# Softmax row sums in an attention kernel: the last key tile of each half is added by VectorE instead of GpSimd

## The reference, cut to what matters

```python
att = jnp.einsum('bhqd,bhkd->bhqk', q, k) * scale     # 16 heads of 64, 1024 queries, 1024 keys
att = jax.nn.softmax(att, axis=-1)                    # divides by the sum of each row over all keys
out = jnp.einsum('bhqk,bhkd->bhqd', att, v)
out = jnp.einsum('bne,de->bnd', out, Wo) + bo
```

## Time and profile before

| what | value |
|---|---|
| median of three executions | 3461.38 us |
| the profiled execution | 3464.02 us |
| span of its trace, first to last instruction | 3462.3 us |
| granted TensorE clock, mean | 0.993 |
| busy: TensorE, GpSimd, VectorE, ScalarE | 98%, 81%, 72%, 47% of the span |

### The profile page before, as it was taken

The page is one execution under the profiler, slowest core; times in us unless marked ns, Lnnn a source line. Parts: engine busy times, 40 slices in busy tenths (PEclk is TensorE's granted clock), DMA queues, the critical chain, the costliest instruction groups (busy, mean ns, idle before and its releaser), DMA issues. The chain is left out here.

```text
span 3462.3 us, 61727 instructions
## 1 busy us (share of the span) xinstructions
PE 3399.4 (98%) x16978; PEld 2088.4 (60%) x16978; DVE 2505.0 (72%) x3133; ACT 1640.8 (47%) x3086; POOL 2794.0 (81%) x2378
## 2 busy tenths in 40 slices
PE   8999799999999999999999999999999999999998
PEld 6888555555555555555555555555555555555698
DVE  8999567777777777777777777777777777777655
ACT  5666344444444444444444444444444444444432
POOL 3333389999999999999999999999999999999511
PEclk9999899999999999999999999999999999999999
DMA  7887756777677777777777677777776677776587
GB/s 246 245 238 240 200 129 160 186 191 187 184 185 186 185 184 182 191 192 189 185 186 187 185 186 186 185 192 187 185 186 186 186 185 181 190 192 155 180 277 251
DMA packets 424594, 669.27 MB, mean 193 GB/s; under 512 B 63585, under 2 KB 229218, under 8 KB 424546
## 3 DMA queue, kind: packets, MB, share of 16 engines
q1 hardware_dynamic: 410210, 645.60, 67.8%
q0 software_dynamic: 14336, 23.08, 3.4%
HBM read 306.98 MB, written 126.12 MB: 125 GB/s over the span
## 5 line engine op out<-in xcount | busy, mean ns | idle before, releaser
L1265 ACT ACTIVATE probs<-psum 128x512 f32<-128x512 f32 x2048 | 1078.1, 604 | 1196.9 <-PE psum L963 1184.9
L1343 DVE TENSOR_REDUCE merged<-psum 128x1 fp32r<-128x1024 f32 x1024 | 1201.1, 1215 | 591.0 <-PE psum L988 585.5
L1597 POOL TENSOR_TENSOR sums<-sums,probs 128x512 f32<-128x512 f32 x762 | 974.3, 1279 | 60.3 <-ACT probs L1265 2.0
L1598 POOL TENSOR_TENSOR sums<-sums,probs 128x512 f32<-128x512 f32 x762 | 979.6, 1286 | 0.0
L1003 PE MATMUL psum<-probs,v_sb 128*64 128x512 f32 x4096 | 935.9, 599 | 0.0
L960 PE MATMUL psum<-q_full,k_full 128*128 128x512 f32 x2048 | 862.2, 421 | 2.5 <-DVE merged L1343 1.6
L963 PE MATMUL psum<-q_rest,k_rest 65*128 65x512 f32 x2048 | 812.3, 397 | 3.4 <-DMA q_rest<-turned 3.4
L1003 PEld LDWEIGHTS psum<-probs,v_sb 128*64 128x64 f32 x4096 | 271.4, 136 | 562.9 <-issue 483.5
L960 PEld LDWEIGHTS psum<-q_full,k_full 128*128 128x128 f32 x2048 | 388.0, 189 | 178.2 <-issue 73.6
L963 PEld LDWEIGHTS psum<-q_rest,k_rest 65*128 65x128 f32 x2048 | 390.1, 190 | 71.0 <-DMA q_rest<-turned 3.7
L1064 PE MATMUL psum<-x_t,w_qk 128*128 128x512 f32 x1536 | 407.9, 402 | 10.2 <-DVE merged L1343 5.9
(11 more groups left out here) (171 smaller groups left out, 3375.0 us busy)
## 6 DMA issues: line engine op xcount, KB each, us to landing
x_t<-xt SPq DMA_DIRECT2D x118, 1024.0 KB, 7.1
k_full<-high SPq DMA_DIRECT2D x256, 256.0 KB
v<-values SPq DMA_DIRECT2D x64, 512.0 KB, 3.3
w_qk<-wqk_parts SPq DMA_DIRECT2D x64, 512.0 KB
v_sb<-v SPq DMA_DIRECT2D x64, 512.0 KB, 5.4
q_full<-high SPq DMA_DIRECT2D x128, 256.0 KB
q_full<-low SPq DMA_DIRECT2D x128, 256.0 KB
k_rest<-low SPq DMA_DIRECT2D x128, 256.0 KB
```

Of the source, the lines that this page charges most:

```text
L1265: nc.scalar.activation(probs[:, kt, h, :], score_bank(j), ACT.Exp, scale=SCALE).then_inc(probs_ready, 1)
L1343: nc.vector.tensor_reduce(out=merged[:, q // GROUP, col:col + 1], in_=work[:, 2 * h:2 * h + 2, :].rearrange("p b c -> p (b c)"), axis=AX, ...
L1597: nc.gpsimd.tensor_tensor(total[:, 0, :], first[:, 0, :], probs[:, kt, 0, :], ALU.add)
L1598: nc.gpsimd.tensor_tensor(total[:, 1, :], first[:, 1, :], probs[:, kt, 1, :], ALU.add).then_inc(sums_added, 1)
```

## The change

GpSimd adds the key tiles 1 to 6 of each half (twelve tiles in a step). Key tile 7 is added by VectorE with one tensor_tensor of 128x1024 for both heads, in a new filler `ADD`, which increments a new counter `sums_full`. `ADD0` (half 0 of this step) stands in group 2 behind NORM1, just ahead of `reduce(s, 5)`; `ADD1` (half 1 of the step before) stands in group 0 behind `low_part`, ahead of `reduce(s, 0)`. `add_up`, ScalarE's overwriting of key tile 7, and SyncE's loads of the last stage wait for `sums_full`. The adds of half 1 of the last step stay as they were.

```diff
-FILLERS = (((), (), ("RECIP0", "RECIP1")),
+FILLERS = (((), ("ADD1",), ("RECIP0", "RECIP1")),
            (("RECIP2", "RECIP3"), ("RAW1",), ("TOKEN0", "TOKEN1", "TOKEN2")),
-           (("NORM0", "SILU0"), ("SILU1", "SILU2"), ("NORM1",)),
+           (("NORM0", "SILU0"), ("SILU1", "SILU2"), ("NORM1", "ADD0")),
            ((), ("RAW0",), ()))
...
+ADDS = KT - 2
...
         def add_up(s, par, fin):
...
-                pe.wait_ge(sums_added, 14 * s)
+                pe.wait_ge(sums_full, 2 * s)
...
         def exp(s, g, i, h):
...
-                added = 14 * s + max(kt, 1) - (0 if g >= 2 else 7)
+                if kt == KT - 1:
+                    counter, added = sums_full, 2 * s + g // 2
+                else:
+                    counter, added = sums_added, ADDS * (2 * s + g // 2 - 1) + max(kt, 1)
                 if not known(added, 1):
-                    act.wait_ge(sums_added, added)
+                    act.wait_ge(counter, added)
...
+            elif name.startswith("ADD"):
+                half = int(name[-1])
+                if is_step(s, NP) or not (fin if half else att):
+                    return
+                p = s - half
+                dve.wait_ge(probs_ready, SCORES * p + 16 * (half + 1))
+                dve.wait_ge(sums_added, ADDS * (2 * p + half + 1))
+                total = sums1[:] if half else sums0[:, par]
+                nc.vector.tensor_tensor(total, total, probs[:, KT - 1], ALU.add).then_inc(sums_full, 1)
...
             for half in range(2) if att else ():
-                for kt in range(1, KT):
+                for kt in range(1, KT - 1):
...
-                        pool.wait_ge(sums_added, 14 * s + 7 * half + kt - 1)
+                        pool.wait_ge(sums_added, ADDS * (2 * s + half) + kt - 1)
```

More of the change, by code:

```diff
@@ L897, in attention_stage @@
     sums_added = sem("sums_added")
+    sums_full = sem("sums_full")
     sum_filled = sem("sum_filled")
@@ L1010, in add_up @@
             if is_step(s, NP):
-                pe.wait_ge(sums_added, 14 * NP - 7)
+                pe.wait_ge(sums_full, 2 * NP - 1)
                 pe.wait_ge(last_sums, 7)
             else:
-                pe.wait_ge(sums_added, 14 * s)
+                pe.wait_ge(sums_full, 2 * s)
             for h in range(2):
@@ L1761, in step @@
                 sp.wait_ge(pv_done, 4 * NP)
-                sp.wait_ge(sums_added, 14 * NP - 7)
+                sp.wait_ge(sums_full, 2 * NP - 1)
                 sp.wait_ge(last_sums, 7)
```

## The result

The changed kernel takes 3589.34 us (median of four executions, 3586.29 to 3589.63), the kernel before 3462.27 us, the median of the three executions named ahead of the prediction and one of 5504.96 us. The ratio is 1.0366, 95% interval 1.0346 to 1.0387: 3.7% slower. The prediction was 3565 us in a range of 3520 to 3605.

What follows compares the result with a forecast made beforehand. TensorE was taken to bound the kernel, at 44.5 us a step. ADD0's 73 us, ADD1's 34 us and -3 us at the end made +104 us, so 3565 us (+3.0%), in a range of 3520 to 3605.

Steps and rivals of the forecast that it cites:

- TensorE sets the pace: Steps of the loop: TensorE never waits for GpSimd, so taking 5.1 us a step off GpSimd is worth 0.
- ADD0 costs 1.2 us a step: Ahead of reduce(s, 5): ADD0 waits for GpSimd's product, delaying the reduction and PJ of group 3; 61 x 1.2 = 73 us.
- ADD1 costs 0.55 us: Ahead of reduce(s, 0): ADD1 waits for the freed GpSimd's first add, delaying add_up's matmuls; 61 x 0.55 = 34 us.
- The end gives 3 us back: Step without projections and last step: 5.3 us can come back, less VectorE's extra add; 3 us taken as gain.
- A: Rival: ADD1 is hidden, ADD0 isn't, as their order hangs on 0.15 us; 3531 us, chance 0.12.
- B: Rival: the adds cost what they cost alone, ADD0 late by 0.7 us, ADD1 hidden; 3501 us, chance 0.08.
- C: Rival: each VectorE add takes 2.30 us, as one in the trace does; 3604 us, chance 0.10.
- D: Rival: no change that can be told (within 0.2%, 7 us), only the end's gain left; 3458 us, chance 0.04.
- E: Rival: faster, GpSimd sets the pace through the buffers of probs; up to 5.1 us a step, 3150 us, chance 0.02.
- the signs named ahead: Profile after: period 46.2 us, ADD0 near 1.75, ADD1 near 2.2, TensorE waits of 1.2 and 0.5, GpSimd idle 3 us.

Runs made afterwards that it cites:

- the relief alone: Kernel before, with key tile 7 of both halves in no row sum (GpSimd adds twelve tiles, VectorE none): 3456.77 us, ratio 0.9983.
- the gather moved: Changed kernel with only GpSimd's copy and gather of the counts moved behind its first key tile of half 0: 3575.08 us, ratio 1.0331.
- both adds moved: Changed kernel with ADD0 between reduce(s, 5) and low_part of group 3, and ADD1 ahead of low_part of group 0: 3461.29 us, ratio 1.000.
- ADD0 moved alone: Changed kernel with only ADD0 moved, to between reduce(s, 5) and low_part of group 3: 3706.03 us, ratio 1.0709.
- the products later: Changed kernel with the expert's three products on GpSimd one key tile later, ahead of tile 4 of half 1: 3657.58 us, ratio 1.0574.
- ADD0 of one head: Changed kernel with ADD0 for head 0 only (128x512), tile 7 of half 0 left out of head 1's sums: 3547.53 us, ratio 1.0258.
- ADD1 alone: Changed kernel, but GpSimd adds all seven tiles of half 0 and VectorE only key tile 7 of half 1: 3507.57 us, ratio 1.0133.

## Why the prediction was right, point by point

**TensorE sets the pace, GpSimd's relief is worth nothing in the loop.** Shown: with the relief alone the period stayed 44.5 us, with all adds off the path too.

**ADD0 costs 1.2 us a step.** Shown: 1.75 us long as worked out, PJ late by 1.12 us and 0.1 us more behind it; alone 77 us over the 61 periods, where the sum had 73. (That the whole time grew by just 73.5 is luck: the end gave 3.5 us back.) That PJ has no slack, and that the price is the rest of GpSimd's instruction and 1.09 us, were shown by a longer instruction (2.30 us, PJ later by 0.55) and a smaller add (1.22 us, PJ earlier by 0.54).

**ADD1 costs 0.55 us, through a collision that the freed GpSimd makes.** The mechanism is shown by the run in which GpSimd keeps its tiles. The term was too small: 0.54 to 0.66 us at the row sums and up to 0.1 us elsewhere, and alone 42 us over the 61 periods in place of 34. Missing from it were the steps in which ADD1 meets the gather: five periods of 48 us, some 1.7 us each above the ordinary, 8 us together. With the gather moved these are gone, and the 61 periods are 7 us shorter.

**The end gives 3 us back.** Wrong in sign: the last 33 us are 3.3 shorter, but step 62 is 5.2 longer. The 3 us are about what the relief alone gave (2.8); the prediction put no cost on step 62, where the relief alone costs 2.0 us and ADD0 comes on top. There NORM1, issued as a GpSimd product ends, lets two adds pass and takes 3.09 us, ADD0 takes 2.29 behind it, and TensorE waits 4.7 us for the reductions:

```profile
3325.06 3.09 DVE L1403 TENSOR_TENSOR out_raw<-out_raw,sum_all 128x512 f32<-128x512 f32 x1
3325.08 1.27 POOL L1611 TENSOR_TENSOR sums<-sums,probs 128x512 f32<-128x512 f32 x1
3326.32 1.28 POOL L1612 TENSOR_TENSOR sums<-sums,probs 128x512 f32<-128x512 f32 x1
3332.68 0.80 PE L962 MATMUL psum<-q_full,k_full 128*128 128x512 f32 x1 [4.66 <-DVE merged L1348]
```

In all, 103.8 us were forecast for the span and 125.4 came. Of the difference, 16.0 us are in the 61 periods (61 x 0.15 = 9.2 from ordinary steps of 1.90 in place of 1.75 us, 8.3 from the long ones, less 1.5 where periods grew by less), 4.9 in the last two steps and 2.1 in the start, and behind the last row sums 1.3 are gained.

**The rivals.** A (ADD1 hidden) turned on 0.15 us; GpSimd came first by 0.13 and 0.05 us, so the order held, which with such a lead was partly luck. Where GpSimd comes later or ADD1 earlier, A is what one sees: 3540 and 3538 us. B (the price alone, 3501 us) falls by the 1.75 and 2.23 us of the adds. The Trainium skill (GPSIMD Engine Reference, section "4.1 Engine selection") advises VectorE for elementwise adds; this case agrees where nothing is in the way (1.22 us for both heads, against 2 x 1.28 on GpSimd), but the advice is about the engine and not about the place. C (2.30 us for each add, 3604 us) is right for ADD1, 2.23 to 2.33 us in ordinary steps, and wrong for ADD0 at 1.75, which meets the shorter product. D and E fall with the runs above; D's time was reached only when both adds were moved. Of the signs named ahead, GpSimd's idle time before half 1 came as well: 3.44 us in the step shown, where 3 were forecast.

## What to carry to other kernels

Before work is moved to an engine with more idle time, ask which of its gaps it falls into and what waits just in time behind that gap: here the same two adds cost 127 us in one place and nothing in another, at a busier VectorE. An engine that is relieved runs earlier, and may so collide with what it never met; a delay that is taken away shifts it too, so that moving one of two harmful adds made the kernel 117 us slower until the other was moved as well. Where TensorE sets the pace and waits at a stretch, look at its granted clock before you sum up the waits: here waits of 1.5 us and more had drops behind them, though not all.

## What the runs showed of the hardware that was not expected

A VectorE add with both inputs in SBUF, issued while GpSimd's indirect gather of the counts was under way, could wait not only for the gather but for the two adds that followed: 3.8 to 4.3 us in place of 1.2. What parted the cases was how far the gather had come. Over the traces of all kernels, the 64 adds of VectorE issued 0.35 to 0.83 us behind the start of that gather all took this long, and the 26 issued earlier (23 as it started, three 0.15 to 0.24 us behind) took 1.18 to 1.26 us. The reason stays open.

Issued while a GpSimd add was under way, VectorE's went in ahead of GpSimd's next instruction in the changed kernel's steps shown: ADD1 1.15 us before the end of the one under way, ADD0 0.68 us before the end of a product. Closer to the end this fails. With both adds moved, ADD0 is issued 0.17 to 0.26 us before a GpSimd add ends, and in 61 steps the next GpSimd add goes first, which makes its 2.51 us:

```profile
1956.91 1.29 POOL L1611 TENSOR_TENSOR sums<-sums,probs 128x512 f32<-128x512 f32 x1
1958.03 2.51 DVE L1386 TENSOR_TENSOR sums<-sums,probs 128x1024 f32<-128x1024 f32 x1
1958.17 1.28 POOL L1612 TENSOR_TENSOR sums<-sums,probs 128x512 f32<-128x512 f32 x1
```

NORM1 in step 62, issued within the last 0.06 us of a product, let two adds pass, in four of the kernels. So a gather isn't needed for two to pass. What decides how many go first stays open.

Such an add also held GpSimd's own gather (1.38 against 1.02 us, where the add came first), and the 128x1 copy ahead of it (up to 1.52 against 0.76 us with both adds moved), though each reads only one word a partition.

The granted clock fell to half after waits of TensorE of 2.1 to 2.4 us in the changed kernel and in nearly each such step with ADD0 moved alone, and after about every second wait of 1.5 us with the products later; after the 0.5 us and 1.1 us waits of the changed kernel's ordinary steps it stayed at 1.00 throughout the loop. But a wait of that length wasn't enough by itself. With ADD0 of one head ADD1 meets the gather as well, and TensorE waits as long:

```profile
2114.36 1.06 PE L1020 MATMUL psum<-sums,ones 128*32 128x512 f32 x8 [2.42 <-DVE sums L1387]
2115.36 3.65 PE L1005 MATMUL psum<-probs,v_sb 128*64 128x512 f32 x16
```

The granted clock is 1.00 from 2114 to 2122 us, `pv` takes its 3.65 us, and the next period is an ordinary one; the trace of ADD1 alone has a wait of 2.42 us like it, at 2992 us. These runs don't show what decides it. Where the clock fell, that cost 1.2 to 2.8 us on top of the wait, from the starts of the matmuls: the row sums and `pv` took 6.23 and 7.42 us to the next quad in place of 4.58, PJ 2.70 us in place of 1.50.
